# A scatter of edge counts that waits, row by row, for another part of the kernel

## Chip, cores and metric

The kernel runs on one core of one Trainium2 chip. The metric is the device time of one execution in microseconds (us).

## What is computed

The input is 3125 nodes with 256 features each, and 53,125 edges sorted by destination. With `xn` the normalised input, the reference adds three things to `x`:

```
edge_index = jnp.stack([src, dst])
xn = _layernorm(x, axis=-1)
x = x + gnn(xn, edge_index, ...) + mix(xn[None], ...)[0]
x = x + ffn(_layernorm(x, axis=-1)[None], ...)[0]
```

`gnn` is three graph convolutions (widths 1024, 512, 256); each is a product with weights and a sum over edges, scaled by degrees, then relu and a layer norm. `mix` is a gated linear attention over eight groups of 32 channels for each node, inside hyperbolic maps (norms, `tanh`, `arctanh`), with a batch norm and a last product. `ffn` is a feed-forward block for the half of the nodes that a router picks.

## The kernel before, in words

The sum over edges is done as a product with a dense matrix of counts. Nodes come in 25 tiles of 125. `counts[t]` holds, for destination tile t, how many edges go from each source node to each of its 125 destinations, in f16, in DRAM. It is cleared first; then the count of each edge is scattered into it, two bytes for each edge.

**The scatter** is GpSimd's work (line 728). The edges lie in 104 rows of 512; each row is four indirect DMAs of 128 edges, so there are 416 in all. Four rows are a group. After the first row of a group, `landing` (lines 716 to 722) waits for the group before it and counts it in the semaphore `landed`. As edges are sorted by destination, tile t needs only the groups up to some number, which VectorE has worked out; SyncE reads it (`landed(t)`) before it fetches `counts[t]`.

**The mixing part** runs at the same time on TensorE, ScalarE and VectorE, in five chunks of 625 nodes. For each chunk TensorE makes six hidden products (`hidden`), ScalarE evacuates each and squares it (`square`, line 1751, semaphore `sq_done`); six products of the spread follow (`spread`), each evacuated (line 1768) and squared too, so there are 12 squares in a chunk and 60 in all. TensorE sums squares to norms and makes four sums of keys (`key_sums`), and VectorE multiplies by each of them (`key`, line 1183 calling 1157, semaphore `qk_done`): four key products in a chunk, 20 in all. Each engine's order is written out by hand; hidden products of the next chunk stand between the steps of this one. Between them stand 26 one-hot batches for the degrees: VectorE compares (lines 909 and 911), TensorE multiplies and counts (`degree`, 16 matmuls a batch).

**The layers** come after the mixing: TensorE waits for all rows of layer 1 (`rows1_ready`), multiplies each fetched `counts[t]` with them (25 matmuls), and does the products of layer 1 and 2 in between. SyncE's queue starts to ask for `landed(0)` only after the residual products of the first four chunks (`res_done`). So scatter and layer 1 may run side by side: a tile needs its groups, not the whole scatter.

Nearly all matmuls show line 2088, a helper; they are told apart by their tiles. After the scatter GpSimd has only small work until layer 1 is under way.

Of the kernel before, what the change touches and what calls it, by code (L numbers as in the profile page):

```python
# [45 lines left out]
assert DC * 128 == ER * EC and sum(DEGREE_RUNS) * DB == DC  # L46
ROWS_A_GROUP = 4
GROUPS = ER // ROWS_A_GROUP
IN_GROUP = EQ * ROWS_A_GROUP
PADE = NWIN * HALO + 4 * HALO  # L50
HUGE = 3e38
# [86 lines left out]
def _build(ctx, nc, a, out, scratch):  # L138
# [7 lines left out]
    def sem(name):  # L146
        if name not in sems:
            sems[name] = ctx.enter_context(nc.semaphore(name))
        return sems[name]
# [23 lines left out]
    at = {"scr": 0, "col": 0, "wm": 0, "big": 0}  # L173
# [149 lines left out]
    for _, k in SEARCH:  # L323
        tables.append(scr[:P, o:o + k].bitcast(I32))
        o += k
# [186 lines left out]
    def _(sp):  # L512
# [51 lines left out]
        def landed(t):  # L564

            groups = sp.value_load(needs[0:1, bass.ds(t, 1)], min_val=1, max_val=GROUPS)
            sp.wait_ge(sem("landed"), groups)
# [88 lines left out]
    def _(pool):  # L656
# [61 lines left out]
        def landing(n):  # L718
            pool.wait_ge(sem(f"scattered{n % 2}"), 16 * IN_GROUP * (n // 2 + 1))
            if n >= 1:  # L720
                pool.wait_ge(sem("landed"), n)
            pool.memset(pool_pause, 0.0).then_inc(sem("landed"), 1)

        for n in range(GROUPS):
            for r in range(n * ROWS_A_GROUP, (n + 1) * ROWS_A_GROUP):
                for g in range(EQ):
                    at_c = g * ER + r
                    pool.indirect_dma_start(cells, bass.IndirectOffsetOnAxis(ap=eidx[:, r * EQ + g:r * EQ + g + 1], axis=0),  # L728
                                            evalue[:, at_c:at_c + 1], None, bounds_check=N * N - 1,
                                            oob_is_err=False).then_inc(sem(f"scattered{n % 2}"), 16)  # L730
                if n >= 1 and r == n * ROWS_A_GROUP:
                    landing(n - 1)
        landing(GROUPS - 1)

# [92 lines left out]
    def _(dve):  # L827
# [92 lines left out]
        def z_low(c):  # L920
            for n, ((into, src), (high, _)) in enumerate(zip(z_parts(c, 1), z_parts(c, 0))):
                dve.wait_ge(sem("zT_done"), 3 * c + n + 1)
                dve.scalar_tensor_tensor(out=into, in0=src, scalar=Z_SCALE, in1=high, op0=ALU.mult,
                                         op1=ALU.subtract).then_inc(sem("zlow_done"), 1)
# [1804 lines left out]
```

## Time and profile before

| | us |
|---|---|
| median of 3 runs | 1814.82 (1813.81 to 1818.94) |
| the profiled execution, its own time | 1807.26 |
| its span in the trace | 1805.4 |
| TensorE busy, matmuls | 1234.7 (68% of the span) |
| VectorE busy | 732.1 (41%) |
| ScalarE busy | 477.4 (26%) |
| GpSimd busy | 538.8 (30%), of it 416.2 in 416 indirect DMAs of line 728 |
| mean granted clock of TensorE | 0.83 |

The span is what the trace covers; the time of the same execution is 1.9 us more. In the trace PE is TensorE's matmul sequence, PEld its weight loads, DVE is VectorE, ACT ScalarE, POOL GpSimd, SP SyncE. Square brackets at the end of a row hold the idle time of the engine ahead of it and what ended it; "issue" means that the profile shows nothing that it waited for, and "remote" a release that the profile can't tie to an instruction. A granted clock of 1.00 is 2.4 GHz, one of 0.50 is 1.2 GHz.

### The profile page before, as it was taken

How to read it: one execution, taken by the hardware profiler on the slowest of the kernel's cores; microseconds unless marked ns; L12 is line 12 of the kernel's file. 1: busy time of each engine (PE TensorE's matmuls, PEld its weight loads, DVE VectorE, ACT ScalarE, POOL GpSimd, SP SyncE). 2: the span in 40 equal slices, each digit the busy share in tenths (PEclk: the TensorE clock that was granted, in tenths of full speed). 3: DMA queues.
4: the chain of work that ended last, by engine and by line, in shares of the span. 5: the costliest groups of instructions: out<-in, count | busy, mean ns of one | idle time of the engine just before them, and what ended most of it. 6: DMA issues, size and time to landing. Idle time of an engine off the chain costs nothing.

```text
span 1805.4 us, 19204 instructions
## 1 busy us (share of the span) xinstructions
PE 1234.7 (68%) x6591; PEld 795.7 (44%) x6591; DVE 732.1 (41%) x1558; ACT 477.4 (26%) x1003; POOL 538.8 (30%) x579
## 2 busy tenths in 40 slices
PE   4973010110001018888999999999999999999796
PEld 4641000000000005555656666666666666566375
DVE  7860020000000007878555545554333233688634
ACT  5340000000011006486332222221211111344164
POOL 3177777766667770000100000021023000000143
PEclk9985555555555558999999999999999999999898
DMA  9820000000000000003132222213333333564311
GB/s 281 283 74 0 0 1 0 0 0 0 0 0 0 1 0 1 1 1 83 48 104 61 73 67 61 58 52 99 87 89 88 78 92 87 141 165 123 91 42 29
DMA packets 82936, 111.25 MB, mean 62 GB/s; under 512 B 51871, under 2 KB 67348, under 8 KB 82872
## 3 DMA queue, kind: packets, MB, share of 16 engines
q1 hardware_dynamic: 62344, 106.98, 21.5%
q0 software_dynamic: 20528, 3.47, 1.4%
q8 instruction: 34, 0.56, 0.1%
q14 instruction: 30, 0.25, 0.0%
HBM read 76.08 MB, written 27.67 MB: 57 GB/s over the span
## 4 chain that ended last, share of the span: by engine, by line
PE 59%; issue 29%; DVE 5%; ACT 4%; another core or an unknown queue 2%; DMA 0%; POOL 0%; DVEq 0%; ACTq 0%; SPq 0%; POOLq 0%
PE psum L2088 58%; PE psum L2468 1%; ACT big L1751 0%; ACT scr L1768 0%; ACT acc L1643 0%; ACT scr L1758 0%; PE psum L2461 0%; ACT scr L1925 0%; ACT scr L1794 0%; DVE big L930 0%; DVE scr L930 0%; DVE scr L1499 0%; DMA scr<-in_src_pad 0%; ACT scr L1775 0%
## 5 line engine op out<-in xcount | busy, mean ns | idle before, releaser
L728 POOL DMA_INDIRECT counts<-big,eidx x416 | 416.2, 1000 | 194.1 <-issue 158.6
L2088 PE MATMUL psum<-rows,scr 125*125 125x512 f16 x1250 | 274.5, 379 | 3.6 <-DVE rows L1299 1.6
L2088 PE MATMUL psum<-big,scr 125*125 125x512 f16 x1250 | 274.6, 379 | 1.0 <-DVE big L1322 1.0
L909 DVE TENSOR_TENSOR acc<-acc,scr 128x2000 bf16<-128x2000 bf16 x26 | 31.2, 1199 | 457.5 <-remote 455.2
L2088 PEld LDWEIGHTS psum<-rows,scr 125*125 125x125 f16 x1250 | 170.2, 136 | 103.3 <-issue 2.9
L2088 PEld LDWEIGHTS psum<-big,scr 125*125 125x125 f16 x1250 | 169.7, 136 | 96.7 <-DVE big L1322 1.5
L2088 PE MATMUL psum<-acc 128*32 128x125 bf16 (+2 forms) x516 | 52.8, 263 | 206.0 <-issue 202.0
L2088 PE MATMUL psum<-wb,scr 128*125 128x512 f16 x600 | 137.0, 379 | 2.0 <-DVE scr L1305 1.4
L2088 PEld LDWEIGHTS psum<-acc 128*32 128x32 bf16 (+1 forms) x516 | 31.9, 121 | 226.6 <-issue 220.0
L2088 PE MATMUL psum<-scr,wm 128*128 128x313 f32 x48 | 22.9, 573 | 140.0 <-ACT scr L1768 110.6
L753 POOL TENSOR_TENSOR acc<-acc,wm 125x256 f32<-125x256 f32 x25 | 17.1, 731 | 319.6 <-DVE acc L1311 319.6
L1768 ACT ACTIVATE scr<-psum 128x626 f32<-128x626 f32 x30 | 20.9, 695 | 338.6 <-issue 280.8
L2088 PEld LDWEIGHTS psum<-wb,scr 128*125 128x125 f16 x600 | 80.8, 136 | 46.8 <-DVE scr L1305 1.9
L2088 PE MATMUL psum<-big,ones 128*32 128x313 f32 (+1 forms) x204 | 36.7, 488 | 81.6 <-issue 76.0
L2088 PE MATMUL psum<-big,wm 128*128 128x313 f16 (+1 forms) x432 | 77.4, 330 | 11.2 <-ACT scr L1758 7.9
L2088 PEld LDWEIGHTS psum<-scr,wm 128*128 128x128 f32 x48 | 11.2, 244 | 153.5 <-ACT scr L1768 114.3
L780 POOL DMA_INDIRECT scr<-picked,eidx x13 | 22.6, 1735 | 181.8 <-issue 181.8
L1388 DVE SCALAR_TENSOR_TENSOR scr<-psum,col,wm 125x512 f32<-125x512 f32 x25 | 18.8, 751 | 128.9 <-PE psum L2088 128.9
L2088 PE MATMUL psum<-wa,scr 128*125 128x512 f16 x300 | 68.9, 379 | 1.8 <-DVE scr L1200 1.1
L834 DVE BATCH_NORM_STATS2 col<-scr 125x6 f32<-125x512 f32 x75 | 49.5, 689 | 45.5 <-ACT scr L1934 28.1
L1305 DVE TENSOR_TENSOR scr<-psum,scr 128x1000 f16<-128x1000 f32 x25 | 30.0, 1199 | 93.5 <-ACT scr L1925 93.5
L2088 PEld LDWEIGHTS psum<-big,wm 128*128 128x128 f16 (+1 forms) x432 | 48.4, 116 | 38.3 <-ACT scr L1758 9.6
(415 smaller groups left out, 1872.6 us busy)
## 6 DMA issues: line engine op xcount, KB each, us to landing
scr<-counts SPq DMA_DIRECT2D x75, 683.6 KB
counts<-wb SPq DMA_DIRECT2D x25, 683.6 KB
counts<-big,eidx POOLq DMA_INDIRECT x416
scr<-counts SPq DMA_DIRECT2D x75, 79.3 KB
scr<-in_x SPq DMA_DIRECT2D x25, 125.0 KB
picked<-big SPq DMA_DIRECT2D x5, 566.6 KB
rows<-in_x SPq DMA_DIRECT2D x5, 560.0 KB
out<-acc SPq DMA_DIRECT2D x5, 560.0 KB
```

What stands on the lines that cost most here:

```text
L728: pool.indirect_dma_start(cells, bass.IndirectOffsetOnAxis(ap=eidx[:, r * EQ + g:r * EQ + g + 1], axis=0), evalue[:, at_c:at_c + 1], None, ...
L753: pool.tensor_tensor(accv[:, t, :], accv[:, t, :], be3r, ALU.add).then_inc(sem("be3_added"), 1)
L780: pool.indirect_dma_start(got[:, g, :], None, picked_dram, bass.IndirectOffsetOnAxis(ap=picked[:, g:g + 1], axis=0), bounds_check=N - 1, o ...
L834: done.did(dve.bn_stats(st2[:, h, :], src[:, h * 512:(h + 1) * 512] if parts > 1 else src))
L909: done.did(dve.tensor_tensor(ohp, free(edp16, b * DB, [[2, DB // 2], [0, P], [1, 2]]), free(iop, 0, [[0, DB // 2], [2, P], [1, 2]]), ALU.i ...
L1305: dve.tensor_tensor(xT16[:, 1].rearrange("p (b k) q -> p b (k q)", b=2), turned_halves(), xT16[:, 0].rearrange("p (b k) q -> p b (k q)", b ...
L1388: dve.scalar_tensor_tensor(out=pre[b][:, 0:D2], in0=bank(b, P, D2), scalar=d2out[:, bass.ds(t, 1)], in1=b2r, op0=ALU.mult, op1=ALU.add).th ...
L1768: act.activation(halves(sTs[c % 2][:, m, :]), pair(m % 2), ACT.Relu if m < 4 else ACT.Copy).then_inc(sem("s_evac"), 1)
L2088: return pe.matmul(o, l, r, start=start, stop=stop)
L2468: last = pe.transpose(bank(5 + k // 4, 128, P, k % 4 * P), pre[0][:, k * 128:(k + 1) * 128], ident[:P, 0:P])
```

## The change

Before each row of the scatter, GpSimd may wait for two semaphores. `KEYS_BY_ROW` lists, for each of the 20 key products, the row that waits for it; `SQUARES_BY_ROW` does so for squares in fours (15 entries, 60 squares). Row 1 waits for 4 squares, row 4 for 8, row 5 for 12, row 6 for one key product, and so on to row 45, which waits for all 20 key products. Rows without an entry don't wait, and no row after 45 does. Nothing else is changed: not the DMAs, their order, the landing counts, or any other engine.

```diff
--- before.py
+++ after.py
@@ -46,6 +46,8 @@
 ROWS_A_GROUP = 4
 GROUPS = ER // ROWS_A_GROUP
+KEYS_BY_ROW = (6, 8, 9, 13, 15, 18, 19, 22, 24, 27, 28, 30, 32, 35, 35, 37, 40, 42, 43, 45)
+SQUARES_BY_ROW = (1, 4, 5, 9, 10, 12, 20, 21, 22, 29, 30, 31, 37, 38, 39)
 IN_GROUP = EQ * ROWS_A_GROUP
@@ -721,8 +723,17 @@
+        def mixing_kept_up(r):
+
+            squares, keys = SQUARES_BY_ROW.count(r), KEYS_BY_ROW.count(r)
+            if squares:
+                pool.wait_ge(sem("sq_done"), 4 * sum(at <= r for at in SQUARES_BY_ROW))
+            if keys:
+                pool.wait_ge(sem("qk_done"), sum(at <= r for at in KEYS_BY_ROW))
+
         for n in range(GROUPS):
             for r in range(n * ROWS_A_GROUP, (n + 1) * ROWS_A_GROUP):
+                mixing_kept_up(r)
                 for g in range(EQ):
                     at_c = g * ER + r
                     pool.indirect_dma_start(cells, bass.IndirectOffsetOnAxis(ap=eidx[:, r * EQ + g:r * EQ + g + 1], axis=0),
```

## Rows read from the trace of the kernel before

**Rows 1.** The page: the span, and the busy share of engines in its 40 slices.

```profile
span 1805.4 us, 19204 instructions
...
PE   4973010110001018888999999999999999999796
...
POOL 3177777766667770000100000021023000000143
PEclk9985555555555558999999999999999999999898
```

**Rows 2.** The table by stage: start and end, length, busy us and instructions (x).

```profile
core 0: us, PE busy (x) PEld busy (x) DVE busy (x) ACT busy (x) POOL busy (x), PEclk, DMA share, GB/s
...
171.00:674.00 503.00, 53.70 (x186) 18.89 (x185) 22.41 (x25) 20.40 (x42) 359.79 (x386) 0.50 0.02 0
...
684.50:853.00 168.50, 151.94 (x997) 98.19 (x997) 138.31 (x209) 117.00 (x245) 0.50 (x2) 0.97 0.08 19
853.00:1223.00 370.00, 365.69 (x1825) 241.16 (x1824) 197.31 (x346) 109.08 (x177) 24.51 (x36) 1.00 0.24 66
```

**Rows 3.** The timeline, both TensorE sequences: start, length, engine, line, instructions.

```profile
300.08 0.26 PE L2088 MATMUL psum<-acc 128*32 128x125 bf16 x1 [1.84 <-issue]
...
301.48 0.10 PEld L2088 LDWEIGHTS psum<-acc 128*32 128x32 bf16 x1 [2.69 <-issue]
...
302.88 0.26 PE L2088 MATMUL psum<-acc 128*32 128x125 bf16 x1 [2.54 <-issue]
```

**Rows 4.** The timeline: TensorE, ScalarE and VectorE inside the scatter.

```profile
161.48 0.68 PE L2088 MATMUL psum<-scr,wm 128*128 128x313 f32 x1 [1.41 <-issue]
...
248.30 0.69 ACT L1768 ACTIVATE scr<-psum 128x626 f32<-128x626 f32 x1 [104.14 <-issue]
...
337.98 1.20 DVE L909 TENSOR_TENSOR acc<-acc,scr 128x2000 bf16<-128x2000 bf16 x1 [101.15 <-remote]
...
382.70 1.22 DVE L909 TENSOR_TENSOR acc<-acc,scr 128x2000 bf16<-128x2000 bf16 x1 [43.19 <-remote]
```

**Rows 5.** The timeline at the end of the scatter: GpSimd and TensorE.

```profile
672.92 0.97 POOL L728 DMA_INDIRECT counts<-big,eidx  x1 [0.30 <-issue]
...
683.12 0.78 PE L2088 MATMUL psum<-big,ones 128*32 128x375 f32 x1 [1.32 <-issue]
684.53 0.84 PE L2088 MATMUL psum<-big,ones 128*32 128x375 f32 x2 [0.63 <-issue]
```

**Rows 6.** The timeline at the start of the scatter: ScalarE and TensorE.

```profile
122.40 0.87 ACT L1758 ACTIVATE scr<-psum,col 128x626 f32<-128x626 f32 x1 [12.29 <-remote]
...
139.64 0.30 PE L2088 MATMUL psum<-acc 128*32 128x125 bf16 x3 [0.47 <-issue]
```

**Rows 7.** The timeline of GpSimd: the first DMAs of rows 0, 10 and 45.

```profile
96.29 2.01 POOL L728 DMA_INDIRECT counts<-big,eidx  x1 [35.51 <-DVE col L1053]
...
155.61 0.97 POOL L728 DMA_INDIRECT counts<-big,eidx  x1 [0.30 <-issue]
...
339.29 1.07 POOL L728 DMA_INDIRECT counts<-big,eidx  x1 [1.02 <-issue]
```

**Rows 8.** The timeline: the 20th square, and key products 5 and 20.

```profile
260.08 0.69 ACT L1751 ACTIVATE scr<-psum 128x626 f32<-128x626 f32 x1
...
686.45 0.80 DVE L1157 SCALAR_TENSOR_TENSOR scr<-psum,scr 128x626 f32<-128x626 f32 x1
...
854.86 0.81 DVE L1157 SCALAR_TENSOR_TENSOR scr<-psum,scr 128x626 f32<-128x626 f32 x1
```

**Rows 9.** The chain of waits in layer 1 (two tiles), and the timeline of its last tile.

```profile
938.10 13.17 PE psum L2088 x61
952.34 13.17 PE psum L2088 x61
...
1199.44 5.56 PE L2088 MATMUL psum<-rows,scr 125*125 125x512 f16 x25
```

**Rows 10.** The waits between 171 and 674 us: total, times, longest.

```profile
POOL counts L728 <- issue: 143.3, 364, 3.2
```

## Prediction, made before any run of the changed kernel

> **What bounds the kernel now.** I read the page first [rows 1]. Its span is 1805.4 us, in 40 slices of 45 us. From the fourth to the fifteenth slice TensorE is nearly idle, its granted clock is at the lower of its levels (0.5, 1.2 GHz), and GpSimd is busy; after them TensorE is busy almost without a break. The table by stage [rows 2] gives the edges. The scatter, 416 indirect DMAs by GpSimd in 104 rows of four, runs from 96 to 674 us [rows 5, 7]. Between 171 and 674 TensorE gets 186 matmuls done in 503 us; between 684.5 and 853 it does 997 in 168.5 us. So some 170 us of mixing work stands behind the scatter, and then 25 tiles of layer 1 behind the mixing.
>
> The timeline inside the scatter [rows 3] shows the form of the slowness. TensorE starts one instruction each 1.40 us (a matmul, a weight load, a matmul), each idle time before it put down to "issue": it waits for nothing that the kernel wrote. What follows is late too [rows 4]: the first pair of matmuls of chunk 1's spread, whose last record starts at 161.48, is seen by ScalarE at 248.30. That is 87 us, or 62 instructions at 1.40 us. VectorE's one-hot batches are released 44.7 us apart, which is 32 x 1.40, and a degree batch is 16 matmuls with 16 weight loads. I read this as a line of about 60 finished but uncounted TensorE instructions, let out one each 1.40 us. I call it the jam.
>
> It belongs to the scatter: it ends just after it [rows 5]. The last indirect DMA is issued at 672.92 and over at 673.89; TensorE still drips until 683.12, and runs freely from 684.53. So a jam takes 10.6 us to clear. It doesn't stand from the start either [rows 6]: the scatter starts at 96 us, and for ScalarE nothing comes from TensorE between 110 and 122.4; then it works again, and from 135 on TensorE thins out for good, with "issue" ahead of each few matmuls (the row at 139.64). A good stretch beside the scatter therefore lasted 14 us (to the first hold-up) or 38 us (to the lasting one).
>
> **The change, part by part.** It adds waits on GpSimd's queue ahead of a row, and no work. GpSimd may issue row r only when the mixing's squares and key products have reached counts. Behind such a wait stand only further rows and the landing counts, which SyncE reads after the mixing; nobody in the mixing waits for GpSimd. The waiting itself I cost at nothing beyond the time waited.
>
> The table asks for 20 squares at row 10 and for the last key product, the 20th, at row 45. Between them 24 rows wait; rows 46 to 103 are free. Before row 10 nothing changes: row 10 is due at 155.61 [rows 7], and its 20th square was made at 260.08 in this run [rows 8], so it binds at once. Rows 15 to 45 ask for key products 5 to 20. At free pace those took from 686.45 to 855.67, or 169 us [rows 8]; 30 rows at 5.25 us (35 rows in 183.7 us [rows 7]) take 158 us. So the table asks for about the pace that the mixing has alone, and scatter and mixing could go side by side if there were no jam.
>
> The sum has a fixed part. Scatter's end as now: 673.9. Clearing: 10.6. What followed the last key product: 1805.4 - 855.7 = 949.7. Together 1634.2 us, to which come the pauses P that the waits put into the scatter, and from which goes C, the part of those 949.7 us that gets done while rows 45 to 103 are issued. The change pays if P - C is under 171.2 us.
>
> P: the first pause, from 155 us on, is the clearing, 10.6 us, and some 1.4 us for the squares asked for, 12 us. From there to the 20th key product I put 193 us of free-running mixing: the 169 us, and an estimate of 24 us for what lies between (five one-hot batches and one quotient block of VectorE). The 35 rows take 184 us, so 9 us of lag must be waited for anyway. The rest are relapses. After a good stretch of G us the jam is back; the scatter goes on to the next waiting row, on average 184/24 = 8 us; there it pauses 10.6 us to clear and 8 us to catch up, 18.6 us. For G = 38, 184/46 = 4 relapses, 74 us, P = 95. For G = 14, 184/22 = 8.4, 155 us, P = 176. Neither row is nearer, so I take the middle, G = 26: 5.4 relapses, 100 us, P = 121.
>
> C: rows 45 to 103 take 334.6 us, from 339.29 to 673.89 [rows 5, 7]. The first G us run freely. In the rest TensorE gets one instruction per 1.40 us and the 62 that it runs ahead: for G = 26, 309/1.4 + 62 = 283 instructions. A tile of layer 1 has 1825/25 = 73 matmuls and as many weight loads [rows 2] and takes 14.24 us [rows 9], so that is 1.9 tiles, 28 us. C = 54 us. G = 38 gives 65, G = 14 gives 42.
>
> Sum: 1634.2 + 121 - 54 = 1701 us of span, beside 1805.4 now. The profiled execution took 1807.3 us by its own time, 1.9 over the span, and the median of the three runs is 7.6 over that: 1710.7, said as **1710 us**. G = 38 gives 1674, G = 14 gives 1778. Layer 1 needs counts in order of tiles, and 45 of 104 rows hold those of the first ten, so no early fetch is late.
>
> Against this change speaks a rule. The trace has TensorE at a matmul per 2.7 us beside the scatter, and at six per us 11 us after it [rows 2, 5]. The Trainium skill, page "SBUF — State Buffer", section "Who interferes with whom", says that a DMA never contends with a compute engine and that only the port pair of VectorE and GpSimd can be fought over. By it holding back DMAs frees nobody; the sum would be that of the third rival. The trace disagrees as far as timing can tell, and I go by the trace.
>
> **The rivals.** (1) *Slower: the jam is back with the first DMA of each burst.* The mixing then advances in pauses alone: P = 193 + 24 x 10.6 = 447, C = 29 (no good stretch), 1634.2 + 447 - 29 = 2052, or 2062 us on the median's scale. For it: between 171 and 674 the jam never lifted by itself, though GpSimd itself stood for up to 3.2 us ahead of a DMA [rows 10]. Against it: two good stretches of over ten us beside the scatter [rows 6], while a burst between two waits is one to three rows, 5 to 16 us. It decides from the point at which a burst carries no mixing: without any clearing cost P is 193, P - C 164, just at break-even. (2) *In between:* bursts carry little, clearing is short: P from 193 to 230, 1808 to 1845 us. (3) *The scatter is not what slows TensorE.* Then each milestone comes when it came before, the 20th key product at 855.7; 59 rows of 5.67 us follow, to 1190 us, and the last tile of layer 1, begun at 1199.44 [rows 9], just finds its counts: 1815 us, the same. Against it is the end of the jam 11 us after the scatter's. (4) *Pacing cures the jam for good*, layer 1 included. Then layer 1 follows the scatter, which ends near 686; its last tile starts at 690 instead of 1199: 1805 - 509 = 1296, or 1305 us. Against it: nothing paces rows 46 to 103, and the jam came at the density of instructions that layer 1 has too.
>
> **How the numbers follow.** Forecast 0.68, with 1670 to 1780 as its own bounds and some way beyond for the parts estimated. Rival 1: 0.13. Rival 2: 0.08, of which 0.03 no change. Rival 3: 0.05, of which 0.03 no change. Rival 4: 0.06. Faster by over 0.3% (what a measurement of this kernel can tell from no change) is 0.68 + 0.06 = 0.74, within it 0.06, slower 0.20. The range leaves out rivals 1 and 4: from 1610, where P is 60 and C 95, to 1830, where a part of rival 2 is in.
>
> **What would show it.** GpSimd's line L728 keeps 416 DMAs, but with idle time put down to ScalarE's squares (L1751) and VectorE's products (L1157), about 120 us in all, and the scatter ends near 795. The 20th key product comes near 460 instead of 855. Between 155 and 460 TensorE shows alternating stretches, with matmuls at free pace and a granted clock that is often at its higher level. After 460 it starts tiles of layer 1, then drips at 1.40 us until some 11 us after the scatter. I'm wrong if the drip fills every burst (rival 1), if it persists in pauses much over 11 us (rival 3), or if layer 1 runs freely beside the scatter (rival 4). A wrong G shows as another number of pauses.

## The result and the profile after

The changed kernel takes **1649.23 us** (median of 4 runs, 1646.55 to 1655.14) beside 1815.85 us before (4 runs, 1813.81 to 1818.94). The ratio is 0.9089, with a 95% interval of 0.9073 to 0.9105: 9.1% faster. The forecast was 1710 us in a range of 1610 to 1830. The profiled execution took 1655.14 us over a span of 1653.3.

The page of the changed kernel (span, then busy tenths of the 40 slices, here of 41.3 us each, and GpSimd's scatter DMAs with count, busy us, mean ns and idle us), to be held against [rows 1]:

```profile
span 1653.3 us, 19208 instructions
...
PE   3975776888300211049999999999999999998896
...
POOL 3155746677777766650000000400230000000334
PEclk9896888899555655569999999999999999999998
...
L739 POOL DMA_INDIRECT counts<-big,eidx x416 | 433.8, 1043 | 231.5 <-issue 143.1
```

TensorE's trough began with the fourth slice before. Now slices 4 to 10 are at 5 to 8 tenths, with the granted clock nearer its higher level (0.87 on average from 157 to 405 us), and the trough is slices 11 to 18. The table by stage (start and end, length, then busy us and instruction count of PE, PEld, DVE, ACT and POOL, the clock, DMA share, GB/s) gives the edges, and answers to [rows 2]:

```profile
97.00:150.00 53.00, 27.38 (x207) 13.90 (x205) 23.33 (x30) 13.32 (x20) 41.83 (x38) 0.76 0.06 16
157.30:405.00 247.70, 192.02 (x1263) 116.96 (x1262) 165.81 (x241) 140.92 (x294) 163.58 (x153) 0.87 0.07 16
405.00:440.00 35.00, 18.69 (x79) 12.86 (x76) 2.98 (x5) 4.01 (x8) 26.70 (x30) 0.73 0.16 37
440.00:733.00 293.00, 40.60 (x105) 19.49 (x105) 12.29 (x24) 9.86 (x24) 204.76 (x224) 0.53 0.03 3
744.00:1078.00 334.00, 328.99 (x1638) 215.79 (x1637) 177.84 (x306) 93.38 (x142) 19.12 (x28) 1.00 0.23 64
```

From 157 to 405 us, beside the scatter, TensorE does 1263 matmuls, 5.1 per us; before, it did 186 in the 503 us up to 674. The jam's sign, idle time that the profile puts down to "issue", comes to 16.9 us in that stretch, beside 341.2 us from 171 to 674 us before (total, times, longest):

```profile
PE psum L2099 <- issue: 16.9, 16, 3.9
```

From 440 to 733 it does 105 matmuls and 105 weight loads in 293 us, one instruction per 1.40 us: the jam, now in layer 1. The timeline shows where the scatter pauses (first DMAs of rows 9 and 20), the last key product, the jam's first drips after it, and the scatter's end:

```profile
157.33 0.97 POOL L739 DMA_INDIRECT counts<-big,eidx  x1 [7.33 <-ACT scr L1762]
...
234.65 1.16 POOL L739 DMA_INDIRECT counts<-big,eidx  x1 [7.59 <-ACT scr L1762]
...
401.75 0.81 DVE L1168 SCALAR_TENSOR_TENSOR scr<-psum,scr 128x626 f32<-128x626 f32 x1
...
430.36 0.38 PE L2099 MATMUL psum<-wm,big 128*125 128x256 f32 x1 [2.43 <-issue]
433.15 0.59 PE L2099 MATMUL psum<-wm,big 128*125 128x256 f32 x1 [2.42 <-issue]
...
728.18 0.97 POOL L739 DMA_INDIRECT counts<-big,eidx  x1 [0.30 <-issue]
...
734.41 0.59 PE L2099 MATMUL psum<-rows,scr 125*125 125x512 f16 x1 [0.83 <-issue]
736.50 2.72 PE L2099 MATMUL psum<-rows,scr 125*125 125x512 f16 x6 [1.50 <-issue]
```

Ten rows wait noticeably: 9, 10, 18, 20, 21, 24, 28, 32, 35 and 42, for 7.33, 4.40, 4.01, 7.59, 4.61, 4.18, 3.71, 5.15, 2.62 and 4.62 us, 48 us together. The 20th key product comes at 401.75 instead of 854.86 [rows 8]; the scatter's last DMA ends at 729.15 instead of 673.89 [rows 5]; the jam clears 7 us after that. The last tile of layer 1 starts its aggregation here, on the timeline of TensorE:

```profile
1046.29 5.56 PE L2099 MATMUL psum<-rows,scr 125*125 125x512 f16 x25
```

In [rows 9] that was 1199.44, or 153 us later, and the span before was 152 us longer. Behind layer 1 nothing changed.

### The profile page after: what moved, and what is told of

The parts are those of the page before. It is cut to its first block, busy times and chain, and to the rows that moved or that the text cites. A ratio compares the mean times of both kernels' runs of the same rounds, so it can differ in the third digit from the quotient of the medians.

```text
span 1653.3 us, 19208 instructions
## 1 busy us (share of the span) xinstructions
PE 1232.8 (75%) x6591; PEld 796.9 (48%) x6591; DVE 732.4 (44%) x1558; ACT 476.6 (29%) x1003; POOL 556.5 (34%) x579
## 3 DMA queue, kind: packets, MB, share of 16 engines
q0 software_dynamic: 20528, 3.47, 1.5%
HBM read 76.08 MB, written 27.67 MB: 63 GB/s over the span
## 4 chain that ended last, share of the span: by engine, by line
PE 66%; issue 19%; DVE 6%; another core or an unknown queue 5%; ACT 4%; DMA 0%; POOL 0%; DVEq 0%; SPq 0%; ACTq 0%; POOLq 0%
PE psum L2099 63%; PE psum L2479 1%; DVE acc L920 1%; ACT acc L1654 0%; DVE scr L1168 0%; PE psum L2472 0%; DVE scr L1510 0%; ACT big L1762 0%; DVE big L941 0%; ACT scr L1779 0%; DVE scr L941 0%; DMA scr<-in_src_pad 0%; DVE scr L1184 0%; ACT scr L1936 0%
## 5 line engine op out<-in xcount | busy, mean ns | idle before, releaser
L739 POOL DMA_INDIRECT counts<-big,eidx x416 | 433.8, 1043 | 231.5 <-issue 143.1
L2099 PE MATMUL psum<-rows,scr 125*125 125x512 f16 x1250 | 283.7, 385 | 34.1 <-issue 31.4
L2099 PE MATMUL psum<-wa,scr 128*125 128x512 f16 x300 | 74.8, 394 | 115.6 <-issue 114.4
L2099 PE MATMUL psum<-big,wm 128*128 128x313 f16 (+1 forms) x432 | 88.9, 362 | 35.0 <-ACT scr L1769 19.2
L2099 PEld LDWEIGHTS psum<-wa,scr 128*125 128x125 f16 x300 | 42.0, 141 | 144.8 <-issue 121.4
L1995 ACT ACTIVATE scr<-scr 125x512 f32<-125x512 f32 x25 | 15.7, 629 | 166.2 <-DVE scr L1399 166.2
L1227 DVE SCALAR_TENSOR_TENSOR acc<-psum,col,scr 125x256 f32<-125x256 f32 x25 | 11.4, 481 | 110.3 <-remote 82.5
L1342 DVE SCALAR_TENSOR_TENSOR scr<-psum,col,wm 125x1024 f32<-125x1024 f32 x25 | 31.9, 1275 | 50.5 <-issue 31.3
L2472 PE MATMUL psum<-ident,scr 125*128 125x125 f32 x50 | 10.2, 287 | 58.6 <-issue 56.7
L1936 ACT CAST scr<-psum 128x1000 f16<-128x1000 f32 x25 | 24.8, 992 | 99.5 <-PE psum L2099 62.4
```

The source lines that it names most:

```text
L1342: dve.scalar_tensor_tensor(out=buf.rearrange("p (h n) -> p h n", h=2), in0=psum[:P, 3:5, :], scalar=y_back[:, bass.ds(t, 1)], in1=b1r.rear ...
L1936: act.copy(xT16[:, 0].rearrange("p (b k) q -> p b (k q)", b=2), turned_halves()).then_inc(sem("xThi_done"), 1)
L1995: act.activation(pre[b][:, 0:D2], pre[b][:, 0:D2], ACT.Relu).then_inc(sem("relu2_done"), 1)
L2099: return pe.matmul(o, l, r, start=start, stop=stop)
```

## Experiments

The kernel before ran beside each group of experiments: 1808.41 us (7 runs) beside e1 to e4, 1807.17 us (7 runs) beside e5 to e8, 1811.86 us (13 runs) beside e9 to e11. Each group had a chip of its own. e12 had a fourth chip, on which the kernel before took another time; that is told there.

Theory A at the start: issuing the scatter's DMAs back to back jams TensorE, a pause clears it. The rivals were that only the start matters, that the writes of counts do it, or that the waits' exact place does.

The distance between DMAs is given in two ways below. The usual distance is the median; it is 1.28 us in the kernel before. The mean distance over a stretch holds the pauses too, also those of the landing counts; in the kernel before it is 1.38 us from 171 to 674 us, and 1.42 us in rows 45 to 103.

**e1: the change's waits up to row 10 only.**

```diff
-KEYS_BY_ROW = (6, 8, 9, 13, 15, 18, 19, 22, 24, 27, 28, 30, 32, 35, 35, 37, 40, 42, 43, 45)
-SQUARES_BY_ROW = (1, 4, 5, 9, 10, 12, 20, 21, 22, 29, 30, 31, 37, 38, 39)
+KEYS_BY_ROW = (6, 8, 9)
+SQUARES_BY_ROW = (1, 4, 5, 9, 10)
```

> Only the waits up to row 10 are kept, so there are the two pauses near 150 and 160 us and none after. Theory A (a jam forms again after some 20 to 40 us beside an unbroken scatter, and only a pause of the scatter clears it): the jam is back before 210 us and stands until 11 us after the scatter; the scatter ends near 687, the mixing is finished long after it, the time is 1780 to 1815 us. Rival B (one clean start past the first hold-up is enough): mixing runs freely to its end near 390 us and the time is at or below the changed kernel's 1649 us.

Measured: 1768.45 us (one run). The table by stage of e1, the same columns:

```profile
160.00:210.00 50.00, 38.83 (x364) 23.90 (x364) 43.41 (x54) 34.85 (x83) 37.71 (x34) 0.93 0.02 2
210.00:680.00 470.00, 59.97 (x216) 21.00 (x211) 20.79 (x23) 21.08 (x38) 337.46 (x364) 0.51 0.02 0
```

After two pauses TensorE runs free for about 50 us (364 matmuls), then the jam is back until the scatter's end, as theory A had it. The time is 12 us under theory A's range. One clean start is worth some 40 us; the pauses after row 10 bring the rest. So the jam does relapse under an unbroken scatter, and the change's gain needs repeated pauses.

**e2: a tiny GpSimd instruction before each DMA of the kernel before.**

```diff
+                    paced()
                     pool.indirect_dma_start(cells, bass.IndirectOffsetOnAxis(ap=eidx[:, r * EQ + g:r * EQ + g + 1], axis=0),
```

paced() is one iota on 128x1 that waits only for the iota eight back.

> The kernel before, with one small iota of GpSimd (0.3 us) ahead of each of the 416 indirect DMAs, and no wait on the mixing; an iota waits only for the one eight back. Theory A (what matters is how densely the scatter's DMAs follow each other, as an overload would have it): at some 1.6 us a DMA instead of 1.28 the jam does not form or lets far more than one instruction per 1.40 us through; the scatter ends near 770 us but mixing and layer 1 run beside it, and the time is under 1600 us. Rival B (what matters is that the scatter stops altogether for some us): the jam forms as before, the scatter is just longer, and the time is 1890 to 1960 us.

Measured: 1738.77 us (one run). The iota was mostly hidden: the DMAs usually stood 1.33 us apart, not 1.6 (1.42 us by the mean of the stretch below), and the last was issued at 690.49. Still the jam leaked:

```profile
171.00:690.00 519.00, 161.00 (x695) 74.08 (x695) 82.36 (x130) 64.26 (x141) 430.34 (x752) 0.56 0.02 1
```

That is 695 matmuls where [rows 2] have 186, in bursts. The size of the edit missed what was meant, so the expectation of either theory wasn't put to the test; what it shows is that an iota ahead of each DMA, and with it 4% more usual distance (3% by the mean), already loosens the jam. Which of the two does it stays open.

**e3: the change, and layer 1 paced in the same way.**

```diff
+TILES_BY_ROW = (47, 50, 53, 56, 58, 61, 64, 67, 69, 72, 75, 77, 80, 83, 86, 88, 91, 94, 97, 99, 102)
...
+            if r in TILES_BY_ROW:
+                pool.wait_ge(sem("agg_done"), 1 + TILES_BY_ROW.index(r))
```

> The changed kernel, with rows 47 to 102 waiting for tiles of layer 1 as well (row 47 for one sum over edges, row 50 for two, to row 102 for 21). Theory A (pauses tied to progress let any work of the other engines run beside the scatter): layer 1 runs at near its own pace, 14.2 us a tile, with pauses of 4 to 8 us; the scatter ends near 810 us instead of 729, layer 1 ends near 860 instead of 1074, and the time is 1430 to 1500 us. Rival B (layer 1 is different, since it fetches counts by DMA and has denser instructions): each tile only moves in pauses, the scatter stretches by about the 22 tiles' 313 us, and the time is within 30 us of 1649 us.

Measured: **1429.28 us** (4 runs, 1424.72 to 1439.03), ratio 0.7896 (0.7874 to 0.7918). This beats both kernels, and lies just below the range of theory A. The stretch that the jam held in the changed kernel, and GpSimd's waits from 405 us on (total, times, longest):

```profile
450.00:790.00 340.00, 298.08 (x1399) 190.87 (x1400) 151.09 (x267) 81.92 (x128) 202.09 (x215) 0.96 0.21 54
```

```profile
POOL counts L742 <- issue: 68.8, 216, 2.3
POOL counts L742 <- PE psum L2102: 61.5, 9, 19.9
POOL counts L742 <- remote: 24.1, 9, 3.0
```

1399 matmuls in 340 us are 4.1 per us, beside 4.9 in the undisturbed layer 1 of [rows 2]. The price is that the scatter's last DMA is issued at 790.48, 62 us later than in the changed kernel, which nothing behind it feels.

**e4: the kernel before, its DMAs bounded so that no count reaches its place.** The counts, and so the sums over the edges, are left out.

```diff
-                                            evalue[:, at_c:at_c + 1], None, bounds_check=N * N - 1,
+                                            evalue[:, at_c:at_c + 1], None, bounds_check=0,
```

> The kernel before, with the bound of the indirect DMAs set to 0, so that the 416 DMAs are issued and counted but write no counts of edges to DRAM (the sums over edges are left out by this). Theory A (the writes of two bytes to DRAM make the jam): no jam, mixing ends near 350 us, layer 1 runs beside the scatter, and the time is under 1350 us. Rival B (the issue of a DMA and its 16 counts on the semaphore make it): the jam stands as before and the time is 1790 to 1830 us.

Measured: 1806.31 us (one run), with 182 matmuls in the stretch of 171 to 674 us, where [rows 2] have 186. What this tells is less than was meant. These are the lines of e4's page on GpSimd's queue and on memory, and then the memory line of e12, which has no scatter DMAs:

```profile
q0 software_dynamic: 20528, 3.57, 1.4%
HBM read 76.08 MB, written 27.67 MB: 57 GB/s over the span
```

```profile
HBM read 76.08 MB, written 27.57 MB: 81 GB/s over the span
```

By the profile e4 wrote as much as the kernel before (27.67 MB), where e12 wrote 0.1 MB less. So the counts didn't reach their places, but it isn't shown that nothing was written. The jam doesn't need the counts to land in their cells; e10 bears on the amount written.

**e5: the change without its waits on squares.**

```diff
-SQUARES_BY_ROW = (1, 4, 5, 9, 10, 12, 20, 21, 22, 29, 30, 31, 37, 38, 39)
+SQUARES_BY_ROW = ()
```

> The changed kernel with its waits on squares left out, so that only the 20 waits on key products (rows 6 to 45) hold the scatter back. Theory A (any wait whose release hangs on TensorE's own line does the work, since it lasts until the line is through): the waits on keys are spread over all rows, so the first of them that falls due behind takes all of the pause, 10 to 20 us instead of 4 to 8, and the time is within 25 us of the changed kernel: 1640 to 1675 us. Rival B (the early waits on squares, at rows 9 and 10, are what keeps the line from forming, and one that has formed is not undone by the later ones): the 20th key product comes late, and the time is 1700 us or more.

Measured: 1666.76 us (2 runs), ratio 0.9221 (0.9190 to 0.9252). Rival B falls, and theory A's range holds. The first wait that bites is long, at row 13, and then the mixing runs:

```profile
192.50 0.97 POOL L739 DMA_INDIRECT counts<-big,eidx  x1 [23.13 <-DVE scr L1168]
```

The jam that stood at row 13 was undone by that one pause. It wasn't the only one: rows 22 and 32 waited 13.4 and 13.5 us, and row 24 waited 7.2. So a jam needn't be prevented, only interrupted, and what the waits on squares add is about 1% of the time (0.9221 beside 0.9089).

**e6: blind pauses in the kernel before, where the change paused.**

```diff
+BLIND_ROWS = (9, 10, 18, 20, 21, 24, 28, 32, 35, 42)
...
+                if r in BLIND_ROWS:
+                    idle(BLIND)
```

BLIND is 30, and idle(n) is n memsets of 128x8 on GpSimd, each waiting for the one ahead.

> The kernel before with no wait on the mixing part: GpSimd instead does 30 tiny memsets, each waiting for the one ahead, before rows 9, 10, 18, 20, 21, 24, 28, 32, 35 and 42, where the changed kernel paused; each pause comes to some 6 to 8 us whatever TensorE does, 60 to 80 us together. Theory A (what counts is that a pause lasts until TensorE's line is empty): a pause that is too short to empty the line once it stands does nothing lasting, so that some stretches are free and others at 1.4 us an instruction; 1690 to 1770 us. Rival B (the pause alone counts, wherever it ends): the mixing part runs as in the changed kernel, the 20th key product is there by 420 us, and the time is 1640 to 1680 us. If no pause of this kind helps, it is 1860 us or more.

Measured: 1657.06 us (2 runs), ratio 0.9167 (0.9133 to 0.9201). The table by stage, the first row to be held against the second row of the changed kernel's:

```profile
157.30:405.00 247.70, 196.97 (x1272) 120.03 (x1271) 164.86 (x240) 143.06 (x297) 185.29 (x416) 0.90 0.09 22
480.00:640.00 160.00, 26.21 (x68) 10.82 (x66) 6.15 (x11) 3.18 (x5) 116.90 (x128) 0.55 0.02 1
```

1272 matmuls beside 1263, and the last key product at 393.99. Theory A, that a pause must last until the line is empty, falls, as far as its forecast of time goes (1690 us and more): pauses that know nothing of TensorE do the same, within 1%. What the change waits *for* hardly matters; that it stops the DMAs now and then does. The trace also parts the DMAs from GpSimd's own busy time: here GpSimd is busy for 185.29 of 247.7 us, 75%, and TensorE is near its free pace; in the jam of [rows 2] GpSimd is busy for 72%.

**e7: three chained memsets before every DMA of the kernel before.**

```diff
                     at_c = g * ER + r
+                    idle(SPACE)
                     pool.indirect_dma_start(cells, bass.IndirectOffsetOnAxis(ap=eidx[:, r * EQ + g:r * EQ + g + 1], axis=0),
```

> The kernel before with three tiny memsets, each waiting for the one ahead, in front of every one of the 416 scatter DMAs, so that they start 1.8 to 2.1 us apart instead of 1.28 us, with no pause longer than that, and the scatter ends at 840 to 970 us. Theory A (the jam comes of the rate at which the DMAs are issued, and needs pauses only because the rate is too high): at the wider spacing TensorE runs free beside the scatter; the mixing part is through by 450 us, layer 1 runs beside the rest, and the time is 1300 to 1450 us. Rival B (any unbroken scatter jams it, at one TensorE instruction for each DMA or so): TensorE lets out one instruction per 1.8 to 2.1 us until the scatter ends, and the time is the scatter's end plus about 1130 us less 174: 1950 to 2100 us. Between them (one instruction still costs 1.4 us but fewer of them are held): some stretches free, 1600 to 1850 us.

SPACE is 3. Measured: 1674.24 us (2 runs), ratio 0.9262 (0.9232 to 0.9293). The number falls into the third case, but its picture is none of the three. The DMAs usually came 2.21 us apart (2.31 by the mean) and the last was issued at 1054.75. Stages, the last key product, TensorE's waits from 440 to 1055 us, and one of them:

```profile
115.00:430.00 315.00, 274.52 (x1750) 174.97 (x1749) 225.91 (x346) 180.45 (x362) 191.81 (x536) 0.95 0.10 26
440.00:1055.00 615.00, 280.11 (x1207) 173.80 (x1207) 127.92 (x227) 67.81 (x105) 359.44 (x1110) 0.74 0.10 25
```

```profile
324.30 0.81 DVE L1165 SCALAR_TENSOR_TENSOR scr<-psum,scr 128x626 f32<-128x626 f32 x1
...
600.93 7.17 PE L2096 MATMUL psum<-rows,scr 125*125 125x512 f16 x25 [18.77 <-DMA scr<-counts]
```

```profile
PE psum L2096 <- DMA scr<-counts: 331.5, 17, 22.8
```

There is no jam anywhere in this trace, and from row 1 to row 18 no two DMAs in turn start more than 3.3 us apart, so no pause did it; the early hold-ups of the other traces, from 113 us on, are gone too. TensorE stands 331.5 us in layer 1, but for tiles of counts that the stretched scatter hadn't delivered. The word "issue" in one trace and "DMA scr<-counts" in the other tell a jam from a missing input. So a wider spacing frees TensorE without any pause, and the bound has moved to the scatter itself.

**e8: e3 with its waits up to four rows earlier.**

```diff
-TILES_BY_ROW = (47, 50, 53, 56, 58, 61, 64, 67, 69, 72, 75, 77, 80, 83, 86, 88, 91, 94, 97, 99, 102)
+TILES_BY_ROW = (46, 48, 51, 53, 56, 59, 61, 64, 66, 69, 72, 74, 77, 79, 82, 85, 87, 90, 92, 95, 98)
```

> The kernel of e3 (the change, and 21 rows that wait for layer 1's tiles) with those waits up to four rows earlier: rows 46, 48, 51, ... 98 in place of 47, 50, 53, ... 102, so that the scatter stops sooner where mixing gives over to layer 1 (there e3's trace had TensorE held up between 420 and 450 us and a pause of 20.9 us at row 53). Theory A (the later part of the time is set by TensorE; what is left of the jam lies in that gap): 10 to 30 us faster than e3, 1400 to 1420 us. Rival B (the gap is layer 1's own start and its DVE chain, which pauses do not shorten): within 10 us of e3's 1429 us. Slower (1440 or more) if the scatter, paused more often, ends so late that something behind it on GpSimd is late.

Measured: 1435.87 us (4 runs), ratio 0.7946 (0.7925 to 0.7967); e3's is 0.7896 (0.7874 to 0.7918). Nothing is gained: rival B.

**e9: the blind pause of e6 before every third row from 9 to 102. e11: ten chained memsets before each row from 9 to 103.**

```diff
+BLIND_ROWS = tuple(range(9, 104, 3))
+BLIND = 30
```

```diff
+BLIND_ROWS = tuple(range(9, 104))
+BLIND = 10
```

The first is e9, the second e11; the rest is e6's.

> The kernel before with the blind pauses of e6 (30 chained tiny memsets, about 5.3 us more than the usual distance between two DMAs) before every third row from row 9 to row 102, 32 of them, 170 us in all, and no wait on any other engine. Theory A (after e6: pauses alone free TensorE, and layer 1 needs them as mixing does): the scatter ends at 673 + 170, some 845 us, mixing is through by 420 us and layer 1 runs near its own pace beside the rest; the time is that of e3 (1429 us) within 30 us: 1400 to 1460 us. Rival B (in layer 1 the waits on finished tiles matter, since they stretch when the line stands): layer 1 stays jammed between pauses as it did in e7, and the time is 1500 to 1680 us.

> The kernel before with ten chained tiny memsets before each row from 9 to 103: about the same total of pauses as e9 (95 of some 2 us, 170 to 210 us), but in small pieces, one behind every four DMAs. Theory A (the mean rate of DMAs decides): as e9 within 30 us. Rival B (a pause must be long enough, about 5 us, for the line to fall): mixing may run free, as with e7's even spacing, but layer 1 is held up for half of the scatter or more, and the time is 1530 to 1700 us.

Measured: e9 1467.24 us (4 runs), ratio 0.8108 (0.8071 to 0.8145); e11 1478.95 us (2 runs), ratio 0.8156 (0.8132 to 0.8181). Stages of e9, then of e11, and e11's waits of TensorE from 560 to 860 us:

```profile
430.00:560.00 130.00, 112.54 (x535) 71.11 (x533) 56.34 (x102) 31.56 (x50) 91.71 (x256) 0.97 0.23 58
560.00:840.00 280.00, 223.92 (x985) 145.16 (x984) 104.48 (x184) 55.41 (x85) 201.65 (x562) 0.89 0.15 36
```

```profile
430.00:560.00 130.00, 126.16 (x628) 82.51 (x627) 68.65 (x121) 34.80 (x53) 89.55 (x245) 1.00 0.18 46
560.00:860.00 300.00, 173.22 (x744) 107.50 (x743) 75.34 (x132) 40.43 (x62) 206.45 (x586) 0.78 0.13 31
```

```profile
PE psum L2098 <- DMA scr<-counts: 126.8, 10, 15.7
```

Two kernels without any wait on the mixing or on layer 1 take 19% and 18% less than the one before. The two are 0.8% apart (by medians) and their intervals touch, so pauses of 2 us after four DMAs do about as well as pauses of 5.3 us after twelve. The mean distance over the scatter is nearly the same, 1.84 us in e11 and 1.79 us in e9: theory A of e11 holds, and a pause needn't be long. In e11 layer 1 is at full pace to 560 us (4.8 matmuls per us) and from then on waits for counts, not for the jam; e9 does fewer matmuls up to 560 us (4.1 per us) and more after it. The two times agree, but not stage by stage. e9 ended 7 us above what was expected; its scatter ends at 842 us.

**e10: half of the edges.** Each DMA takes 64 of its 128 partitions; the other edges' counts are left out.

```diff
-                    pool.indirect_dma_start(cells, bass.IndirectOffsetOnAxis(ap=eidx[:, r * EQ + g:r * EQ + g + 1], axis=0),
-                                            evalue[:, at_c:at_c + 1], None, bounds_check=N * N - 1,
+                    pool.indirect_dma_start(cells, bass.IndirectOffsetOnAxis(ap=eidx[:64, r * EQ + g:r * EQ + g + 1], axis=0),
+                                            evalue[:64, at_c:at_c + 1], None, bounds_check=N * N - 1,
```

> The kernel before, each scatter DMA given 64 of its 128 partitions: half of the edges are left out of the counts. The 416 DMAs stay. Theory A (the load is per DMA: its issue and its completion counts): GpSimd still starts one per about 1.28 us, TensorE still lets out one instruction per 1.40 us, and the time is 1780 to 1815 us. Rival B (the load is per packet or descriptor): with half of them the line drains, TensorE runs free for most of the scatter, and the time is below 1500 us. If the DMAs get shorter in step (0.7 us each), the scatter ends by 450 to 500 us and the jam with it; then the pace of TensorE inside it tells the two apart (1.4 us: per DMA or per time; half of it: per packet).

Measured: 1821.89 us (8 runs), ratio 1.0050 (1.0035 to 1.0065), with 188 matmuls from 171 to 674 us. GpSimd's DMA and the packets of its queue (count, MB, share):

```profile
L728 POOL DMA_INDIRECT counts<-big,eidx x416 | 385.5, 927 | 223.5 <-issue 188.0
```

```profile
q0 software_dynamic: 20528, 3.41, 1.3%
```

That is 7 us over theory A's range; rival B falls. Half the elements change nothing. But the queue still counts 20528 packets, as many as in the changed kernel, so this separates elements from DMAs, not packets from DMAs. The number of packets in all doesn't jam TensorE either. In the kernel before, the scatter's queue has 11648 packets from 171 to 674 us, 23 per us; from 1223 to 1500 us another queue has 27654, 100 per us, and TensorE is busy for 274.53 of 277 us (each queue's packets, MB and share, and the stage):

```profile
q0 software_dynamic: 11648, 0.12, 1.7%
```

```profile
q1 hardware_dynamic: 27654, 24.99, 36.1%
1223.00:1500.00 277.00, 274.53 (x1405) 184.02 (x1404) 92.29 (x210) 51.91 (x101) 28.31 (x26) 1.00 0.36 91
```

**e12: no scatter DMA at all.** Seven chained memsets stand in place of each; counts, and so the sums over edges, are left out.

```diff
-            pool.wait_ge(sem(f"scattered{n % 2}"), 16 * IN_GROUP * (n // 2 + 1))
...
-                    pool.indirect_dma_start(cells, bass.IndirectOffsetOnAxis(ap=eidx[:, r * EQ + g:r * EQ + g + 1], axis=0),
-                                            evalue[:, at_c:at_c + 1], None, bounds_check=N * N - 1,
-                                            oob_is_err=False).then_inc(sem(f"scattered{n % 2}"), 16)
+                    idle(7)
```

> The kernel before with each of the 416 scatter DMAs replaced by seven chained tiny memsets on GpSimd (about 1.2 us, as long as a DMA's turn): the counts, and so the sums over the edges, are left out; GpSimd stays as busy for as long. Theory A (the DMAs are what holds TensorE, not GpSimd being busy): TensorE runs free from 110 us on, the 20th key product is there by 400 us and 949.7 us follow it as in the trace of before; the time is 1290 to 1360 us, the floor that pauses can approach. Rival B (GpSimd's own instructions and their semaphore counts hold TensorE up, whatever they do): TensorE at one instruction per 1.4 us until about 650 us, and the time is 1750 to 1850 us. A part of both (some stretches held up in layer 1, as in e7, where three such memsets stood before each DMA): 1400 to 1600 us.

Measured: 1272.06 us (2 runs), **and the kernel before, on the same chip, 1289.13 us** (3 runs, 1287.53 to 1289.59; granted clock 0.98, beside 0.83 on the three other chips); ratio 0.9870 (0.9836 to 0.9905). On this fourth chip the kernel before is, with all its 416 DMAs, 1.3% slower than with none, which leaves no room for a jam worth naming; no trace of it there is on record. So e12 can't say whether the DMAs or GpSimd being busy hold TensorE up; e6 says that, where GpSimd was busier (75% beside 72%) and TensorE ran near its free pace. What e12 gives is the floor, on that chip:

```profile
span 1271.8 us, 21284 instructions
...
PE   2998798898998999999999999999999899987995
```

```profile
321.93 0.81 DVE L1160 SCALAR_TENSOR_TENSOR scr<-psum,scr 128x626 f32<-128x626 f32 x1
```

The last key product is at 321.93, as in e7 (324.30), and 949 us follow it. The changed kernel wasn't run on that chip.

## Why the forecast held, and where it missed

- **The jam belongs to the scatter, relapses, and a stop of the DMAs ends it**: right, on the chips where there is one. It clears 7 us after the scatter in the changed kernel (forecast 10.6). e3, e6, e7, e9 and e11 each move the time by changing only when the DMAs are issued; all but e3 do it with memsets on GpSimd.
- **The fixed part**, 673.9 + 10.6 + 949.7 = 1634.2 us, holds in its last term: in e12, where nothing disturbs layer 1, 1271.8 - 322.7 = 949.1 us follow the last key product. The 10.6 were 7.35, from 729.15 to 736.50.
- **P, the pauses, forecast 121 us, was 55** (729.15 - 673.9). This is the step that failed. Row 45 was issued 66 us later than before (405.27 beside 339.29), and the rows from there on took 323.9 us instead of 334.6, a gain that no term held. "Before row 10 nothing changes" was off as well, with no harm: row 9 waited for its 16 squares, and rows 9 and 10 together waited 11.7 us, where 12 were forecast for the first pause. What was wrong is the price of the relapses. The prediction took each relapse to cost 10.6 us of clearing and 8 us of catching up, 5.4 times. No pause reached 10.6 us; none had to. There was no full relapse while the scatter was paced: from 157 to 405 us TensorE's idle time put down to "issue" is 16.9 us in all and 3.9 us at most, and the "alternating stretches" that the prediction named aren't there. The blind pauses of e6 and e11 show that nothing has to wait for the line; DMAs that are rarer on average are enough. From row 9 to row 42 the changed kernel issues 132 DMAs in 387.62 - 157.33 = 230.3 us, 1.74 us each. By the mean, too, e6 has 1.83 us in these rows and e3 1.62 us from 450 to 790 us, both near free pace, and e7's 2.31 us is wholly free. The kernel before is jammed at 1.38 us, and at 1.42 us in its rows 45 to 103; e2 leaks at 1.42 us. So the edge lies between 1.42 and 1.62 us, on these chips and for this stream; it wasn't narrowed, and e2 beside the kernel before shows that the mean isn't all of it.
- **G, the length of a good stretch, taken as 26 us**: 50 us in e1, some 22 us after row 45 in the changed kernel (the timeline's drips begin by 428, the last key product is at 402). The first lies beyond the prediction's ends of 14 and 38. The term was right in kind, and with no relapse between the pauses it mattered only after row 45.
- **C, forecast 54 us, was 36**: 1634.2 + 55.2 - 1653.3 = 36, which includes the 3 us by which the clearing was shorter. The rows agree: 79 + 105 = 184 matmuls behind the mixing's last key product, at 73 a tile, are 2.5 tiles of 14.24 us, 36 us. The good stretch gave 79 of them, 15 us' worth, where 26 us were counted; it was shorter, and TensorE did only 2.3 per us in it. The rest gave 105, 20 us, where 28 were counted; 6 of these were the 62 instructions that TensorE was said to run ahead. Nothing of them shows: the 105 matmuls and their weight loads are what one per 1.40 us gives in 293 us.
- **The sum**: P came out 66 us lower and C 18 us lower, together 48 us, which is 1701 less 1653 of span. The misses have opposite signs in the sum and partly hid each other. That the forecast came within 4% is in part luck.
- **Rival 1** (jam back at each burst) fell with the first bursts: 1263 matmuls in 157 to 405 us are more than pauses of 48 us in all can hold. **Rival 2** asked for P of 193 us and more; it was 55. **Rival 4** (pacing cures the jam for good) is false for this change, since rows 46 to 103 aren't paced, and right for the mechanism: paced throughout, e3 comes to 1429 us, 124 us above that rival's 1305. **Rival 3** (the scatter isn't what slows TensorE) is false on three chips; but on the fourth the same DMAs cost 17 us, of 1289. The rule of the Trainium skill, page "SBUF — State Buffer", section "Who interferes with whom", that a DMA never contends with a compute engine, fits that chip alone, and there within 1.3%; on the three others a stream of DMAs held TensorE up, by which path is open.
- **The 20th key product**, forecast near 460, was there at 402; in e7 at 324. The change leaves 78 us in the mixing alone. Over half of it goes before row 9, where no wait yet holds the scatter back: from 97 to 150 us the changed kernel does 207 matmuls, e12 454 and e7, on a chip with the jam, 453. 247 matmuls at the 5.9 per us of e12's next 200 us are 42 us, an estimate.

**Open.** What in a DMA jams TensorE: not the landing of counts in their cells (e4), not the number of elements (e10), not the number of packets per us as such (the counts under e10); its issue, its kind of packets or its completion signals are left. Whether the profiler has a part in it: every run on record, on every chip, has a span and a granted clock from the profiler, so no run shows the kernel without it. Why one chip of four shows nothing of it. That TensorE's line is of some 62 finished instructions was only read from [rows 4] and not tested. A spacing just past the edge, about 1.5 us by the mean from the first DMA on, wasn't tried; it would end the scatter near 100 + 416 x 1.5 = 724 us, an estimate, and might keep e7's early mixing.

## What to carry to other kernels

When an engine drips at a fixed pace with "issue" ahead of each instruction, look at what another queue does at a like pace, and thin that out: idle instructions between the DMAs of a long scatter brought 18 to 19% here with no dependence on anybody's progress, and 21% with waits. Then ask at once who needs what is now late: e7 slowed the scatter too much, waited 331.5 us for its result, and kept 7%. And run the kernel before on more than one chip before building on such an effect.

## What the runs showed of the hardware

- On three chips a stream of GpSimd's indirect DMAs, usually 1.28 us apart, held TensorE to one instruction per 1.40 us; at 2.21 us apart not at all. With an iota between them and 4% more usual distance (e2, one run) 3.7 times as many matmuls came through.
- It isn't the number of packets: 23 per us went with the jam, 100 per us of another queue with TensorE busy for 99%.
- GpSimd hid a 0.16 us iota nearly whole between two DMAs (1.28 to 1.33 us), while three chained memsets cost 0.93 us.
- Halving an indirect DMA's partitions shortened it on GpSimd only from 1000 ns (the page of before) to 927 ns, and left its packets as they were.
- The kernel before ran at 1289 us on one chip (3 runs within 2.1 us) and at 1803 to 1819 us on all others.
